# Decoder layer on one core: the two halves of the summed squares added by an accumulating DMA, in a new hand-written order

## What is computed

```python
# A, self attention (per head; K=32 heads, H=8 channels each, M=4 angles)
z = silu_or_linear(causal_conv4(x @ in_proj_w))          # values, gate, score
p = exp(clip(score) - slope * distance)
re, im = cumsum(p*v*cos(theta*v), T), cumsum(p*v*sin(theta*v), T)
den = cumsum(p, T)
y = rms_norm([re, im] / den) @ [W_re, W_im] * gate
x1 = layernorm(x + y @ out_proj_w)
# B, cross attention: autocorrelation by FFT, top 5 lags, softmax, roll
x2 = layernorm(x1 + autocorrelation(x1, ctx) @ Wo)
# C, two branches of 8 experts of rank 64 with softmax weights
prod = (x2 @ V) * cumsum(x2 @ W, T) * weights
out = layernorm(x2 + prod @ U / n_valid)
```

## Time and profile before

| | before |
|---|---|
| timed runs (3), median | 986.42 us |
| lowest, highest | 985.76, 988.19 us |
| the profiled execution | 987.52 us |
| its span, first to last instruction | 985.7 us |
| TensorE busy | 880.5 us, 89% |
| VectorE busy | 759.7 us, 77% |
| ScalarE busy | 543.3 us, 55% |
| GpSimd busy | 96.1 us, 10% |
| DMA packets and bytes | 45994, 50.65 MB |

### The profile page before, as it was taken

How to read it: one execution, slowest core, us unless ns; L and a number is a source line. 1 busy time by engine, 2 the same in 40 slices (tenths; PEclk the granted TensorE clock), 3 DMA queues, 4 the chain that set the end, 5 groups by cost and what they waited for, 6 DMA issues and landing times.

```text
span 985.7 us, 11073 instructions
## 1 busy us (share of the span) xinstructions
PE 880.5 (89%) x3738; PEld 532.0 (54%) x3738; DVE 759.7 (77%) x1285; ACT 543.3 (55%) x884; POOL 96.1 (10%) x160
## 2 busy tenths in 40 slices
PE   0559974999999999899999999999999998997896
PEld 0234642554675556564766465555665574656345
DVE  3667899699988998789988897899879895373231
ACT  0557658575757374766567573957375655311310
POOL 0002201100120003100210012000210023001000
PEclk9869995999999999999999999999999999999899
DMA  5906013310342006110611043101520060000000
GB/s 143 248 20 128 19 47 59 71 64 1 65 86 65 0 12 118 43 44 1 128 44 44 0 78 94 44 1 28 102 65 0 1 129 22 1 1 21 1 0 22
DMA packets 45994, 50.65 MB, mean 51 GB/s; under 512 B 19415, under 2 KB 39410, under 8 KB 45938
## 3 DMA queue, kind: packets, MB, share of 16 engines
q0 software_dynamic: 6912, 25.17, 13.5%
q1 hardware_dynamic: 39026, 24.77, 9.0%
HBM read 20.57 MB, written 4.19 MB: 25 GB/s over the span
## 4 chain that ended last, share of the span: by engine, by line
PE 69%; DVE 15%; ACT 10%; issue 3%; POOL 2%; SPq 2%; DMA 0%; ACTq 0%; DVEq 0%; POOLq 0%
PE ps L812 11%; PE ps L793 11%; PE ps L784 10%; PE ps L673 5%; PE ps L613 4%; PE ps L750 4%; PE ps L598 3%; PE ps L717 3%; PE ps L643 3%; PE ps L466 3%; PE ps L727 2%; DVE zc L2522 2%; DVE sc L2601 2%; ACT L1423 2%; PE ps L801 1%
## 5 line engine op out<-in xcount | busy, mean ns | idle before, releaser
L2601 DVE TENSOR_TENSOR_SCAN sc<-mask,sc 128x1024 f32<-128x1024 bf16 x64 | 146.2, 2284 | 0.5
L784 PE MATMUL ps<-cum,mw 128*128 128x512 f32 x256 | 122.1, 599 | 0.0
L793 PE MATMUL ps<-x2t,mv 128*128 128x512 f32 x256 | 121.4, 597 | 0.0
L812 PE MATMUL ps<-up,prod 128*128 128x256 f32 x512 | 116.4, 380 | 1.4 <-DVE prod L2835 0.9
L812 PEld LDWEIGHTS ps<-up,prod 128*128 128x128 f32 x512 | 94.8, 190 | 17.5 <-issue 5.6
L2341 POOL DMA_DIRECT2D acc<-sq x48 | 41.9, 874 | 587.4 <-ACT sq L1572 587.4
L1668 ACT ACTIVATE cs<-ps 128x512 f32<-128x512 f32 x64 | 38.0, 594 | 98.0 <-PE ps L784 98.0
L2593 DVE TENSOR_TENSOR sc<-sc,g 128x1024 f32<-128x1024 f32 x64 | 77.3, 1207 | 9.2 <-ACT sc L1556 9.2
L2522 DVE SCALAR_TENSOR_TENSOR zc<-ps,cw,zc 128x510 f32<-128x510 f32 (+2 forms) x96 | 71.2, 741 | 11.2 <-ACT zc L1485 8.9
L784 PEld LDWEIGHTS ps<-cum,mw 128*128 128x128 f32 x256 | 46.9, 190 | 59.8 <-issue 57.9
L598 PE MATMUL ps<-xt,win 128*128 128x512 f32 x128 | 66.3, 644 | 8.9 <-DVE zc L2522 8.9
(11 more groups left out here) (265 smaller groups left out, 1524.5 us busy)
## 6 DMA issues: line engine op xcount, KB each, us to landing
acc<-sq POOLq DMA_DIRECT2D x48, 512.0 KB, 4.6
xa<-in_x_dram SPq DMA_DIRECT2D x8, 512.0 KB, 4.3
xs_a<-in_x_dram SPq DMA_DIRECT2D x8, 512.0 KB, 3.6
cin<-in_ctx_dram SPq DMA_DIRECT2D x8, 512.0 KB, 4.5
out_dram<-prod SPq DMA_DIRECT2D x8, 512.0 KB, 2.9
prod<-in_L_ffn_V_fwd_dram SPq DMA_DIRECT2D x2, 256.0 KB
prod<-in_L_ffn_W_fwd_dram SPq DMA_DIRECT2D x2, 256.0 KB
prod<-in_L_ffn_W_inv_exp_dram SPq DMA_DIRECT2D x2, 256.0 KB
```

Of the source, the lines that this page charges most:

```text
L784: last = mm(o, mw[:, t, br, c:c + P], cum[:, t, :], start=(t == 0), stop=(t == 1))
L793: last = mm(o, mv[:, t, br, c:c + P], x2t[:, t, :], start=(t == 0), stop=(t == 1))
L812: mm(d, prod[:, j, q * P:(q + 1) * P], up[:, j, :], start=(j == 0), stop=False)
L2601: V.tensor_tensor_scan(flat, mask[:, 0:2 * T], flat, 0.0, ALU.mult, ALU.add)\
```

## The change

The addition of the two halves leaves VectorE. GpSimd issues it as one more accumulating DMA per tile and chunk, which adds `acc[:, h, 1, :]` into `acc[:, h, 0, :]` (128x512, 256 KB) once the three adds of 512 KB have landed. `added[h]` now counts four landings per chunk and tile instead of three, and TensorE's `a_squares` waits for it directly instead of for VectorE.

```diff
-              + each("p2 g both gf y", range(2)) + each("frac mom scan", range(UNITS))
+              + each("p2 g gf y", range(2)) + each("frac mom scan", range(UNITS))
@@ TensorE, a_squares
-                    pe.wait_ge(*VEC_A.at(i, "both", h))
+                    pe.wait_ge(added[h], 16 * M * (i + 1))
@@ ScalarE, a_squares
-                        act.wait_ge(added[h], 16 * ((M - 1) * i + m - 1))
+                        act.wait_ge(added[h], 16 * (M * i + m - 1 - (m == 1)))
@@ GpSimd
-                    pool.wait_ge(added[h], 16 * ((M - 1) * i + m - 1))
+                    pool.wait_ge(added[h], 16 * (M * i + m - 1))
...
+            @staged
+            def a_both(i, h):
+
+                pool.wait_ge(added[h], 16 * (M * i + M - 1))
+                G.dma_start(acc[:, h, 0, :], acc[:, h, 1, :], accum_op=ALU.add).then_inc(added[h], 16)
@@ VectorE
-            @staged
-            def a_both(i, h):
-
-                dve.wait_ge(added[h], 16 * (M - 1) * (i + 1))
-                TT(acc[:, h, 0, :], acc[:, h, 0, :], acc[:, h, 1, :], ALU.add).then_inc(*VEC_A.tick("both", h))
```

Besides, the order of the steps is another one on all five queues (594 steps on TensorE and 611 on ScalarE, the same ones as before; VectorE has 569 instead of 585, GpSimd 89 instead of 73). The parts of it that matter here, for the start:

```diff
@@ TensorE
             a_project(0, 3)
+            a_sums(0, 0)
+            a_sums(0, 1)
             fold(0)
-            a_sums(0, 0)
...
@@ VectorE, chunk 0 to 2
             biases()
-            a_both(0, 0)
-            a_both(0, 1)
             a_weight(0)
-            b_fold(0, "cf")
...
             a_conv(1, 2)
-            b_products(0)
-            b_heads(0)
+            b_fold(0, "cf")
             a_conv(1, 3)
-            b_topk(0)
+            b_fold(0, "xf")
...
             a_scan(1, 6)
+            b_products(0)
             a_moments(1, 7)
+            b_heads(0)
             a_scan(1, 7)
-            b_residual(0, 0)
-            b_residual(0, 1)
+            b_topk(0)
+            b_weight(0)
+            b_apply(0)
+            b_mix(0)
             b_fold(1, "cf")
-            a_both(1, 0)
-            a_both(1, 1)
             a_weight(1)
             a_factor(1)
             a_heads(1, 0)
             a_heads(1, 1)
+            b_residual(0, 0)
+            b_residual(0, 1)
+            a_residual(1, 0)
+            a_residual(1, 1)
+            a_scores(2)
+            a_conv(2, 0)
             c_cum(0)
```

More of the change, by code:

```diff
@@ L845, in _ @@
             fold(17)
-            a_sums(0, 2)
+            a_sums(0, 3)
+            a_squares(0)
+            a_factor(0, 0)
+            a_factor(0, 1)
+            a_transpose(1, 0)
+            a_transpose(1, 1)
+            a_scores(1)
+            a_out(0, 0)
+            a_project(1, 0)
             fold(18)
+            a_out(0, 1)
+            a_project(1, 1)
             fold(19)
             fold(20)
+            a_spread(1, 0)
             fold(21)
             fold(22)
-            a_sums(0, 3)
+            a_spread(1, 1)
+            a_project(1, 2)
             fold(23)
             fold(24)
-            a_squares(0)
             fold(25)
@@ L1113, in _ @@
             b_out(3, 1)
-            a_out(4, 0)
             a_transpose(5, 0)
             a_transpose(5, 1)
-            b_transform(4, "cf", 0)
+            a_out(4, 0)
+            a_scores(5)
             a_out(4, 1)
-            a_scores(5)
             a_project(5, 0)
@@ L1314, in _ @@
             a_sums(7, 1)
+            b_back(6, 0)
+            b_back(6, 1)
             c_out(5, 0)
+            c_out(5, 1)
             b_out(6, 0)
-            c_out(5, 1)
             b_out(6, 1)
@@ L1735, in _ @@
             fold(12)
-            a_angles(0, 6)
-            a_squares(0, 4)
-            a_angles(0, 7)
-            a_squares(0, 5)
             fold(13)
             fold(14)
+            a_norm(0)
+            a_transpose(1, 0)
+            a_transpose(1, 1)
             fold(15)
             fold(16)
+            a_scores(1)
+            a_exp(1)
+            a_project(1, 0)
             fold(17)
-            a_squares(0, 6)
-            a_squares(0, 7)
+            a_project(1, 1)
             fold(18)
             fold(19)
+            a_turns(1, 0)
+            a_turns(1, 1)
+            a_linear(1, 0)
+            a_linear(1, 1)
+            a_angles(1, 0)
+            a_turns(1, 2)
             fold(20)
@@ L1751, in _ @@
             fold(22)
+            a_angles(1, 1)
+            a_turns(1, 3)
             fold(23)
-            a_norm(0)
-            a_transpose(1, 0)
-            a_transpose(1, 1)
             fold(24)
             fold(25)
-            a_scores(1)
-            a_exp(1)
-            a_project(1, 0)
             fold(26)
             fold(27)
+            a_project(1, 2)
             fold(28)
-            a_project(1, 1)
             fold(29)
+            fold(30)
             a_layer(0)
-            fold(30)
             fold(31)
@@ L1884, in _ @@
             a_squares(2, 7)
-            b_back(1, 0)
-            b_back(1, 1)
+            a_norm(2)
             c_layer(0)
-            a_norm(2)
             b_layer(1)
+            a_transpose(3, 0)
+            a_transpose(3, 1)
+            a_scores(3)
             c_transpose(1, 0)
@@ L1892, in _ @@
             b_transform(2, "cf", 0)
-            a_transpose(3, 0)
-            a_transpose(3, 1)
-            a_scores(3)
+            b_transform(2, "cf", 1)
             a_exp(3)
@@ L2925, in _ @@
             a_fraction(1, 7)
-            b_apply(0)
-            b_mix(0)
             a_scan(1, 5)
@@ L2977, in _ @@
             c_prod(0, 3)
-            a_scan(2, 2)
+            b_topk(1)
+            b_weight(1)
             c_scale(0, 4)
             c_prod(0, 4)
-            b_topk(1)
+            a_scan(2, 2)
+            a_moments(2, 3)
             c_scale(0, 5)
             c_prod(0, 5)
-            b_weight(1)
+            b_apply(1)
+            b_mix(1)
             c_scale(0, 6)
             c_prod(0, 6)
-            a_moments(2, 3)
             a_fraction(2, 5)
@@ L3019, in _ @@
             a_conv(3, 0)
+            c_cum(1)
+            b_fold(2, "xf")
             a_split(3)
             a_den(3)
-            b_fold(2, "xf")
             a_conv(3, 1)
@@ L3161, in _ @@
             a_residual(4, 0)
+            a_scores(5)
             a_residual(4, 1)
-            a_scores(5)
-            c_cum(3)
             a_conv(5, 0)
@@ L3170, in _ @@
             a_fraction(5, 1)
+            c_cum(3)
             a_poly(5, 0)
-            b_fold(4, "xf")
+            c_softmax(3)
+            c_normalise(3)
+            c_split(3)
             a_poly(5, 1)
```

888 lines of the change are left out of this document (433 added, 455 removed).

## The result

The changed kernel takes 994.16 us (median of 8 runs, 991.74 to 996.67) against 987.50 us (8 runs) of the kernel before, run beside it: a ratio of 1.0061, 95% interval 1.0038 to 1.0084. It is slower by 0.6%, some 6 us (6.7 between these two medians). The forecast was plus 6 us, 992.4 us: the sign is right and the size nearly so. The profiled execution took 993.1 us around a span of 991.3 us, 5.6 more than before.

A forecast was written before the change was run, and what follows sets the result against it. VectorE's in-order chain was taken to set the pace while the pipeline fills, TensorE from 187.33 us on. The terms 0 + 0 + 8 - 2 gave plus 6 us on 986.42, 992.4 us; 8-in-10 range 978 to 1000.

The forecast's parts named there:

- Part 1: VectorE's 16 additions of the halves go: booked 0 in the middle, ceiling 10.9 us.
- Part 2: The addition as GpSimd's accumulating 256 KB DMA, landing in 3.3 us ahead of `a_squares`: booked 0, bound 10 us.
- Rival 3: TensorE waits for the DMA at `a_squares` in most chunks, 10 us on top: 1002 us; chance 0.08.
- Part 3: New order while the pipeline fills: C of chunk 0 starts later, 8 us of new TensorE idleness (3 to 13).
- round trip bare: TensorE, ScalarE, TensorE trip that `b_apply` waits for, without other work in between: estimated 3 us, before 8.8.
- step (c): On VectorE, chunk 0's B steps go behind `a_scan(1, 7)`, `b_residual(0, .)` behind chunk 1's heads, `c_cum(0)` behind `a_scores(2)`.
- Step (a): On TensorE, `fold(0)` moves behind `a_sums(0, 1)`; 7.43 us of work from 60.4 to 72.5 us comes later.
- Part 4: Rest of the order, after the start: lighter VectorE and later TensorE give 2 us back, ceiling 12.8.
- the middle's 12.8 us of idleness: TensorE's idle time from about 187.3 to 817 us, the most the later order could give back.
- Rival 1: The fill is free, C starts before 197 us and the middle gives 6 us back: 980 us; chance 0.25.

The follow-up runs named there:

- the DMA alone: Against the kernel before: old order on every queue, halves added by DMA right behind the last 512 KB add instead of by VectorE; 1009.20 us, ratio 1.0217.
- `rstd` let through: Old order with the halves added by DMA, but in five chunks the first rstd group issued between the two new DMAs; 1000.69 us, ratio 1.0126.
- rest only: No DMA, VectorE adds where data land; order of the kernel before up to `a_squares(2)`, the changed kernel's from there; 981.05 us, ratio 0.9930.
- the new order with early additions: The changed kernel's order on every queue, no DMA, each addition on VectorE placed where its data land; 991.40 us, ratio 1.0048.
- the new start only: No DMA, VectorE adds where data land; the changed kernel's order up to `a_squares(2)`, that of the kernel before from there; 1004.49 us, ratio 1.0158.
- the old start with the DMA: The changed kernel with its DMA, but with the order of the kernel before up to the middle of C of chunk 0; 996.75 us, ratio 1.0085.

## Why the prediction was right, and where it was not

**Part 1 (0 for VectorE's additions): right**, by the run without them, 0.9998 of the time, and in the new order as well.

**Part 2 (0 for the DMA, the middle covered): right for the new order**, 1.1 us between the medians, with waits of 0.78 and 0.85 us in chunks 5 and 6. From the last 512 KB issue to `a_squares` it was 6.5 to 7.6 us in the old order, and the new one leaves 8.7 to 10.3 in chunks 2 to 7, into which the chain nearly fits (8.3 to 9.1 where it was exposed, in the DMA alone). Two terms were mis-sized. The landing was 4.0 us in the median (3.3 to 5.4), not 3.3; in the DMA alone it was 3.6. And "in the same order TensorE would stall by 0.9 us in such a chunk, 7 us over eight" was 11.2 us with `rstd` let through: it was read off chunk 2, where 7.2 us lie between issue and `a_squares`, while chunks 4 and 5 had 6.7 and 6.5 and waited 2.3 and 2.6. It left out most of what the DMA alone did: 0 was booked for GpSimd's queue "with 3 us as the bound". That holds in the new order, but in the old one the hold cost 8.5 us, more than the whole forecast. I had named the `rstd` groups behind the waiting DMA, but not what stands behind their reader on ScalarE (`c_layer`, then a table load and `a_norm`), nor that TensorE's `c_transpose(0, .)` stood ahead of `a_squares(1)`. The new order has `a_norm(2)` ahead of `c_layer(0)` and `a_squares(1)` ahead of `c_transpose(0, .)`, and in chunks 3 and 5 an `rstd` ahead of the waiting DMA. Rival 3's price of 1002 us would have been too low if the exposure had been that of the old order, where the kernel takes 1009.

**Part 3 (the start costs 8): right in its stations, and its size partly by another path.** Forecast and found: idle ahead of `a_sums(0, 1)` about 10, 12.1 us; last scan of chunk 1 ends at 173.4, 173.6; round trip bare 3, 3.5; `a_weight(1)` 187.0, 187.56; `b_residual(0)` complete 198, 198.05; `a_scores(2)` 201 to 203, 202.63; C's first hidden matmul 204.7 to 206.6, 206.07; TensorE's idleness up to there 77, 76.3. The loss at the ruler of chunk 2 is 8.8 us, but the 8 were booked as idleness alone, and there only 6.6 us are idleness. The other 2.2 us are longer busy time for as many matmuls, and the sum had no term for that. The clock fits: from the granted share in stretches of about 1 us and TensorE's busy time in them I estimate 14.8 us lost to the half clock up to chunk 2, against 11.5 before. The comparison that tests it as a cause, without any DMA, is the new order with the old and with the new start: 981.05 against 991.40 us, some 10 us (each beside its own kernel before, 987.48 and 987.96). That shows the start as a whole, all that stands ahead of `a_squares(2)`. Which step of it costs is not isolated: the stations fit step (c), `b_residual(0)` behind the heads, but no run puts that step alone back. Step (a), the late folds, isn't confirmed as a cause: more idleness before 98 us is there, but moving it away again helped no station.

**Part 4 (2 back): right in sign, too small, and not by the path given.** The changed kernel's trace has 3.2 us; without the DMA and with the old start it is 6.4 (981.05 against 987.48 us). It was booked out of the middle's 12.8 us of idleness. But of the 2.8 us that the changed kernel wins there 0.1 is idleness (11.7 to 11.6 us between chunks 2 and 7), and of rest only's 5.0 it is 1.9. The rest is shorter busy time, some 1.7 us of it the clock fall that the trace before has and these have not.

**The sum** of 6 thus stood on 8 and minus 2, where the runs have about 9 to 10, minus 3 to minus 6, and 0 to 1. Both terms were too small and the errors cancel, and both left out the clock; that the sum came out as near as it did is partly luck. Rival 1 fell at its own condition: C started at 206, not before 197.

## What to carry over

Count a new wait by what is queued behind it, two engines deep: here, in the old order, the new landing cost 8.5 us through the queue that issued it, beside the 12.5 that were left with its reader. In this filled pipeline with one full engine, work taken off another was worth nothing in either order, while a start that delays the last stage by 19 us costs about what the full engine can't bring forward. Look at the clock in stretches of a few us before calling two stretches alike: 1.00 over 500 us hid 3.4 us at half clock. And when an order is searched as a whole, time its pieces: the later part of this one was worth 6.4 us, the start cost some 10.

## What the hardware showed that I had not expected

**Behind short waits of TensorE the clock can fall, and that can cost more than the waits.** In the tail of the DMA alone TensorE waits 0.74, 2.44 and 0.78 us between 831 and 838 us, where before it waits 0.66, 0.78 and 0.34 in the same place and its clock stays at 1.00. After the longer waits the clock is granted at half (1.2 of 2.4 GHz) for between 6 and 7 us:

```profile
832.00:836.00 4.00, 2.48 (x22) 1.87 (x17) 0.42 (x1) 3.91 (x8) 1.21 (x2) 1.00 0.33 113
836.00:840.00 4.00, 2.31 (x10) 1.94 (x11) 2.76 (x5) 2.81 (x6) 0.00 (x0) 0.68 0.07 22
840.00:844.00 4.00, 4.00 (x12) 3.27 (x11) 0.41 (x1) 2.48 (x3) 0.00 (x0) 0.50 0.00 0
844.00:848.00 4.00, 4.00 (x11) 1.97 (x11) 1.44 (x3) 0.88 (x2) 0.00 (x0) 0.97 0.00 0
```

At half clock 6 us of matmuls do what 3 us would, so some 3 us are lost there. A second fall follows from 953 to 957 us, which the kernel before does not have, some 1.7 us more as an estimate. Over the whole tail the DMA alone is busy for 5.3 us longer and idle for only 1.2 us longer:

```profile
831.40:1006.60 175.20, 150.57 (x540) 91.23 (x540) 63.31 (x141) 47.49 (x80) 9.80 (x21) 0.93 0.03 10
```

The kernel with the new start only shows such a fall behind waits of 0.78 and 1.81 us (0.50 and 0.61 from 303 to 309 us), and the old start with the DMA behind 3.03 us (0.50 and 0.54 from 259 to 265 us). The length of a wait doesn't tell by itself: the kernel before loses the clock in chunk 6 behind 0.39, 0.78 and 0.31 us and keeps it in the tail behind 0.66, 0.78 and 0.34, and the DMA alone keeps it behind waits of 2.35 and 2.45 us in chunks 4 and 5.

**An accumulating DMA from SBUF to SBUF lands late.** 256 KB took 4.0 us (3.3 to 5.4), 512 KB 4.7. The Trainium skill (DMA: Bandwidth & Descriptors, Anatomy of one DMA) would give 2.6 and 3.2 us as an estimate; the measurement decides, and half the bytes save only 0.7 us of 4.7 (in the DMA alone 1.0 of 4.6).

**The clock varies from run to run.** Runs of one kernel differ by up to 7 us, in most kernels along with the mean granted clock: the new order with early additions took 990.57 to 990.77 us at 0.965 and 996.11 to 996.22 at 0.956. Kernels with the old start and no DMA stayed at 0.962 to 0.968, and the others reached down to 0.951. But the kernel before also spread over 5.5 us, with 0.963 in its slowest runs and 0.967 in some near its median, so the mean clock does not order the runs by itself. Why it differs from run to run isn't shown.
